# Turning both quantised activations by DMA in a fused attention and FP4 feed-forward kernel

## What is computed

```python
def fp4_quant_dequant(x):
    xb = x.reshape(shape[:-1] + (shape[-1] // BLOCK, BLOCK))
    scale = jnp.maximum(jnp.max(jnp.abs(xb), axis=-1, keepdims=True) / 6.0, 1e-12)
    idx = jnp.searchsorted(_MID, jnp.abs(xb / scale))
    return (_GRID[idx] * jnp.sign(xb / scale) * scale).reshape(shape)
...
# attention: a decaying linear attention, chunked in the reference
v = out32 @ W_write.T
intra = einsum(S * M, v)        # S[i, j] = x[i] . x[j-1], M = decay and causal mask
x = _layernorm(x + out + alpha * (reads @ W_read.T))
# feed-forward, each matmul on quantised operands; H = 256, I = 704
gate, y = fp4_linear(x, w_gate), fp4_linear(x, w_up)
h = jax.nn.silu(gate) * y
x = _layernorm(x + fp4_linear(h, w_down))
```

## Time and profile before

| | |
|---|---|
| median of 3 runs | 324.36 us (324.16 to 324.38) |
| span of the profiled execution | 322.5 us |
| PE, PEld busy | 314.5 us (97%), 285.2 us (88%) |
| DVE busy | 293.0 us (91%) |
| POOL busy | 238.2 us (74%) |
| ACT busy | 213.2 us (66%) |
| DMA | 15.7 MB, 14% of the 16 engines' time |
| granted TensorE clock | full in all 40 slices |

### The profile page before, as it was taken

One profiled execution on the slowest core, in us unless ns is written; L12 is line 12 of the kernel. 1 busy time (PEld: TensorE's weight loads), 2 busy tenths in 40 slices (PEclk: granted clock), 3 DMA queues, 4 the chain that ended last, 5 costly groups with the idle time before them and its releaser, 6 DMA issues.

```text
span 322.5 us, 6519 instructions
## 1 busy us (share of the span) xinstructions
PE 314.5 (97%) x2067; PEld 285.2 (88%) x2067; DVE 293.0 (91%) x746; ACT 213.2 (66%) x521; POOL 238.2 (74%) x258
## 2 busy tenths in 40 slices
PE   7999999999999999999999999999999999999994
PEld 3999988989998998999989998898989889998983
DVE  4799789989899999899998999889999999999973
ACT  7769994767775647844784556766675555665664
POOL 1999898668696868676886768777779588368872
PEclk9999999999999999999999999999999999999999
DMA  6830301010010200320020200021000000001002
GB/s 227 302 125 9 132 0 67 1 66 2 1 67 16 84 16 0 100 82 3 16 83 17 83 17 3 33 65 35 1 18 17 16 18 17 19 16 35 17 33 84
DMA packets 8242, 15.69 MB, mean 49 GB/s; under 512 B 1040, under 2 KB 5136, under 8 KB 8208
## 3 DMA queue, kind: packets, MB, share of 16 engines
q1 hardware_dynamic: 7920, 15.01, 14.0%
q10 hardware_dynamic: 288, 0.26, 0.3%
HBM read 11.08 MB, written 4.19 MB: 47 GB/s over the span
## 4 chain that ended last, share of the span: by engine, by line
PE 69%; DVE 17%; issue 5%; ACT 4%; POOL 3%; ACTq 0%; DVEq 0%; POOLq 0%
PE gu L1712 11%; PE gu L1716 11%; PE gu L1713 11%; PE bank L1817 5%; PE bank L1712 4%; PE bank L1716 4%; PE bank L1713 4%; PE bank L1722 3%; DVE h_y L1094 3%; PE bank L1725 3%; PE bank L1726 3%; DVE w_raw L1209 2%; DVE hqT_lo L1236 2%; DVE h_am L1215 2%; PE bank L1783 2%
## 5 line engine op out<-in xcount | busy, mean ns | idle before, releaser
L413 POOL TENSOR_TENSOR h_q<-h_g,h_ns 128x704 f32<-128x704 f32 x32 | 51.2, 1604 | 47.7 <-DVE h_g L1099 47.6
L1712 PE MATMUL gu<-guT_hi,xqT_hi 128*128 128x512 f32 (+1 forms) x192 | 74.0, 386 | 0.7 <-DVE w_raw L1209 0.6
L1713 PE MATMUL gu<-guT_lo,xqT_hi 128*128 128x512 f32 (+1 forms) x192 | 72.2, 376 | 0.0
L1716 PE MATMUL gu<-guT_hi,xqT_lo 128*128 128x512 f32 (+1 forms) x192 | 56.6, 376 | 0.0
L699 ACT ACTIVATE w_raw<-gu 128x512 f32<-128x512 f32 x64 | 29.3, 462 | 32.7 <-PE gu L1716 32.4
L406 POOL TENSOR_TENSOR h_n<-w_raw,h_rs 128x704 f32<-128x704 f32 x32 | 47.0, 1472 | 3.4 <-DVE h_rs L1089 3.2
L719 ACT CAST hqT_hi<-bank 128x512 fp32r<-128x512 f32 x64 | 30.4, 478 | 17.7 <-PE bank L1817 17.2
L1712 PEld LDWEIGHTS gu<-guT_hi,xqT_hi 128*128 128x128 f32 x192 | 36.1, 188 | 6.0 <-ACT xqT_hi L688 0.9
L1716 PEld LDWEIGHTS gu<-guT_hi,xqT_lo 128*128 128x128 f32 x192 | 35.5, 188 | 6.0 <-ACT xqT_lo L693 0.2
L1713 PEld LDWEIGHTS gu<-guT_lo,xqT_hi 128*128 128x128 f32 x192 | 36.1, 188 | 4.8
L1094 DVE SCALAR_TENSOR_TENSOR h_y<-h_sq,h_n 128x704 f32<-128x704 bf16 x34 | 36.9, 1090 | 0.0
(11 more groups left out here) (159 smaller groups left out, 936.7 us busy)
## 6 DMA issues: line engine op xcount, KB each, us to landing
xs<-in_x_rows_dram SPq DMA_DIRECT2D x8, 512.0 KB, 3.4
out_dram<-wq_gu SPq DMA_DIRECT2D x32, 128.0 KB, 1.7
x_full<-in_xt_rows_dram SPq DMA_DIRECT2D x7, 512.0 KB, 3.2
w_raw<-in_w_ffn_dram SPq DMA_DIRECT2D x6, 352.0 KB, 6.0
w_pair<-in_w_attn_dram SPq DMA_DIRECT2D x1, 512.0 KB, 5.2
x_full<-in_xt_rows_dram SPq DMA_DIRECT2D x1, 256.0 KB, 2.6
x_full<-in_xt_rows_dram ACTq DMA_DIRECT2D x1, 256.0 KB, 3.4
scal<-in_scalars_dram ACTq DMA_DIRECT2D x1, 1.0 KB, 1.7
```

The lines of the kernel that those rows point to most:

```text
L413: nc.gpsimd.tensor_tensor(blocks(h_q[:, p, 0:I]), blocks(h_g[:, p, :]), per_block(h_ns[:, p, :], HB), ALU.mult).then_inc(h_quant, 1)
L1712: nc.tensor.matmul(dst, lh, rh, start=(first and i == 0), stop=False)
L1713: nc.tensor.matmul(dst, lh, rl, start=False, stop=False)
L1716: last = nc.tensor.matmul(dst, ll, rh, start=False, stop=(end and i == len(terms) - 1))
```

## The change

1. **Grids turned by DMA.** The grid values that `x_to_grid` and `h_to_grid` make are now bfloat16 (`x_g`, `h_g`). For all x and for h of tiles 0 to 29, SP issues a transposing DMA from `x_g` or `h_g` to `x_gT` or `h_gT`. The block scales (`x_ns`, `h_ns`) go their own way: PE transposes them in one instruction (`x_scale_rows`, `h_scale_rows`: 40 or 56 rows), ACT copies them from PSUM (`copy_x_scales`, `copy_h_scales`), SP writes them to DRAM and reads them back with each row repeated over 16 partitions (`x_sT`, `h_sT`). POOL multiplies grid by scales already in the turned layout (`x_spread`, `h_spread`), and ACT and DVE round and subtract from SBUF, over 768 columns at once for h (`h_round_all`, `h_rest_all`). Tiles 30 and 31 still go through `h_dequant` and `h_transpose`.
2. **Squares in PSUM.** `x_squares`, `h_squares` and `w_squares` write float32 to PSUM banks; the two DVE helpers read them there.
3. **Scale rows of odd length**, padded to 5 and 7 groups (`XC`, `SC`), and `x_moments` works on one column at a time (four instructions in place of two). `out_moments` leaves `o_nm` out; POOL folds it into `o_shift`.
4. **The last scores block of a batch** (j = 3, 128 columns) is two plain float32 matmuls on `x_full` in place of six fp32r ones; the next load of `x_full` waits for it.
5. **v and x rests** of the first batches are always made by DVE; `v_subtract`, `xq_subtract` and the ACT copies behind them are gone.
6. **Everything is reordered**: PSUM banks by tables indexed by batch or tile, no loop body, a new list on every engine. `gate_up` waits for `silu_ready` first and for `h_ready` before its second bank.

```diff
-            def v_subtract(n, u):
-            def xq_transpose(n, u, free):
-            def xq_subtract(n, u):
+        s_at = ((6, 3, 5, 4),
...
+            def write_h_scales(k, p, turn):
+                sp.wait_ge(hs_copied, k + 1)
+                sp.dma_start(h_scales_dram[k], h_s[:, p, :]).then_inc(hs_written[p], 16)
+            def spread_h_scales(k, p, turn):
+                sp.wait_ge(hs_written[p], 16 * turn)
+                if turn > 1:
+                    sp.wait_ge(h_quant, k - 1)
+                sp.dma_start(h_sT[:, p, :], over_rows(h_scales_dram[k], SC, HC)).then_inc(hs_landed[p], 16)
+            def turn_h_grid(k, p, turn):
+                sp.wait_ge(hg_repeated, k + 1)
+                if turn > 1:
+                    sp.wait_ge(h_quant, k - 1)
+                sp.dma_start_transpose(h_gT[:, p, :, :], h_g[:, p, :]).then_inc(hg_turned[p], 16)
...
             def load_x_transposed(n):
                 sp.wait_ge(xT_lo_ready, 2 * n)
+                sp.wait_ge(s_filled, 4 * n)
...
+            def h_spread(k, p, turn):
+                pool.wait_ge(hs_landed[p], 16 * turn)
+                pool.wait_ge(hg_turned[p], 16 * turn)
...
+                nc.gpsimd.tensor_tensor(h_q[:, p, :], h_gT[:, p, :, :].rearrange("p c t -> p (c t)"), h_sT[:, p, :],
+                                        ALU.mult).then_inc(h_quant, 1)
...
-                nc.scalar.activation(h_sq[:, p, :], h_n[:, p, :], ACT.Square, scale=ROOT_K).then_inc(h_square, 1)
+                nc.scalar.activation(two_banks(h_sq_at[k]), halves(h_n[:, p, :]), ACT.Square,
+                                     scale=ROOT_K).then_inc(h_square, 1)
...
-                nc.vector.tensor_scalar(z_nm[:, c], z_sum[:, c], -1.0 / D, None, ALU.mult)
...
+                for i in (2 * u, 2 * u + 1):
+                    nc.vector.tensor_scalar(z_nm[:, i:i + 1], z_sum[:, i:i + 1], -1.0 / D, None, ALU.mult)
...
+            def h_rest_all(k, p):
+                dve.wait_ge(hT_hi_ready, 2 * k + 2)
+                nc.vector.tensor_tensor(hqT_lo[:, p, :], h_q[:, p, :], hqT_hi[:, p, :].bitcast(F32),
+                                        ALU.subtract).then_inc(hT_lo_ready, 2)
...
+                if j == TILES - 1:
+                    prev, cur = slice(j * P - 1, (j + 1) * P - 1), slice(j * P, T)
+                    for dk in range(DK):
+                        last = nc.tensor.matmul(ps[:, s_at[n][j], 0:P], x_full[:, dk, prev], x_full[:, dk, cur],
+                                                start=(dk == 0), stop=(dk == DK - 1))
...
+            def h_scale_rows(k, p, free):
+                pe.wait_ge(hs_repeated, k + 1)
+                wait_all(free)
+                nc.tensor.transpose(ps[0:SROWS, hs_at[k], 0:P], h_ns[:, p, :], ident[:]).then_inc(hs_filled, 1)
```

More of the change, by code:

```diff
@@ new lines, in _ @@
+            decay_scores(3, 2)
+            h_magic_add(4, 0)
+            h_reciprocals(6, 0)
+            h_rest_all(0, 0)
+            h_magic_add(5, 1)
+            h_rest_all(1, 1)
+            hidden(7, 1, 0)
+            hidden(7, 1, 1)
+            v_rest(3, 1)
+            h_maxima(7, 1)
+            h_to_grid(4, 0)
+            h_to_grid(5, 1)
+            h_divisors(7, 1)
+            h_reciprocals(7, 1)
+            x_residual(3, 0)
+            hidden(8, 0, 0)
+            hidden(8, 0, 1)
@@ new lines, in _ @@
+            h_to_grid(8, 0)
+            v_rest(4, 0)
+            h_magic_add(9, 1)
+            h_to_grid(9, 1)
+            x_maxima(3, 1)
+            x_residual(4, 0)
+            x_divisors(3, 1)
+            hidden(11, 1, 0)
+            x_reciprocals(3, 1)
+            xq_rest(3, 0)
+            x_moments(4, 0)
+            hidden(11, 1, 1)
+            out_residual(2, 2)
+            h_maxima(11, 1)
+            x_magic_add(3, 1)
+            out_moments(2, 0)
+            h_rest_all(4, 0)
@@ new lines, in _ @@
+            x_moments(4, 1)
+            out_residual(4, 0)
+            xq_rest(3, 1)
+            hidden(12, 0, 0)
+            hidden(12, 0, 1)
+            h_magic_add(10, 0)
+            h_maxima(12, 0)
+            h_to_grid(10, 0)
+            out_moments(4, 0)
+            h_divisors(12, 0)
+            h_reciprocals(12, 0)
+            hidden(13, 1, 0)
+            decay_scores(5, 0)
+            h_magic_add(11, 1)
+            x_maxima(4, 1)
+            hidden(13, 1, 1)
+            x_divisors(4, 1)
@@ new lines, in _ @@
+            out_residual(6, 2)
+            h_reciprocals(14, 0)
+            h_rest_all(8, 0)
+            xq_rest(4, 0)
+            h_to_grid(12, 0)
+            v_rest(5, 0)
+            out_moments(6, 0)
+            hidden(15, 1, 0)
+            v_rest(5, 1)
+            hidden(15, 1, 1)
+            x_residual(5, 0)
+            h_maxima(15, 1)
+            decay_scores(5, 2)
+            h_magic_add(13, 1)
+            x_moments(5, 0)
+            h_to_grid(13, 1)
+            hidden(16, 0, 0)
```

2523 lines of the change are left out of this document (1502 added, 1021 removed).

## The result

The changed kernel takes 354.19 us (351.41 to 354.80) where the kernel before, on the same chip, takes 324.37: a ratio of 1.090, 95% interval 1.086 to 1.094. It is 29.8 us slower, where 302 was predicted. The profiled execution has a span of 352.8 us. All times are medians of a kernel's executions, and where one execution was over 1.5% slower than the kernel's fastest, the median without it is 0.2 to 1.5 us lower (loads first 349.5, split scores block 350.0, no turns 326.3, no round trip 318.8, writes by ACT 350.0).

What follows compares the result with a forecast made beforehand. PE was taken to bound the kernel, with DVE leading after the change: DVE busy 286.3, with idle start and end 299.4, plus 1 between, plus 1.9 to the runs' median, gave 302 us; range 295 to 316.

Steps and rivals of the forecast that it cites:

- PE's work: On PE, removed and added transposes, scores block and subtractions sum to -25.0 us, up to -28 with small ones.
- the bound's 0.1 us for a change of kind: On PE, 46 scale transposes might each also pay about 0.1 us between other matmuls: +10 instead of +5.1.
- The new contacts: On DVE, 46 subtractions now reading two SBUF operands wait on POOL, 0.27 us each: +12.4 us.
- The squares' term: On DVE, squares in PSUM take away the waits on POOL in the passes for h and x: -14.7 us.
- DVE leads: The forecast case: DVE's busy time plus its idle time sets the span, giving 302 us; chance 0.48.
- slack towards PE: DVE's 16.4 us of idle time between start and end, expected to shrink to 0.5 to 2 us.
- PE leads: Rival: DVE's contacts stay near 4 us and PE sets a span of 295 to 297.5, time 298; chance 0.17.
- SP and DMA: Turns land in 3 us, scales' write and read take 1.7 + 2.6; no cost while DVE's distance covers them.
- The load of `x_full` ... covered by the batch's `gate_up`s: On SP, this load now waits for the fourth scores block; its 3 us were to be hidden behind gate_up work.
- The turns are late: Rival: at 5 us a half of x comes 2 us late, some six of 16 halves, 12 us: 314; chance 0.15.
- The rival of serial turns: Transposing DMAs run one after another, each as slow as the slowest load: 331 us; chance 0.10.
- the three signs named: Signs against the forecast: DVE's or POOL's largest wait for a DMA, PE gaps over 10 us, first gate_up later.

Runs made afterwards that it cites:

- loads first: Changed kernel with the second batch's load of x_full put behind four weight loads and the load of xs in SP's list: 350.16 us.
- split scores block: Changed kernel with each batch's last scores block as split terms again, so no load of x_full waits for the fourth block: 350.21 us.
- no turns: Changed kernel with x_full's second load behind the other loads and all 46 transposing DMAs left out: 326.79 us.
- no round trip: Changed kernel with x_full's second load behind the other loads and the scales' 46 DRAM writes and 46 reads left out: 320.32 us.
- writes by ACT: Changed kernel with x_full's second load behind the other loads and the 46 scale-row writes issued by ACT, not SP: 351.23 us.
- the kernel that comes nearest (316.55): Changed kernel with x_full's second load moved back, an eighth of the scale reads' bytes, and the old last scores block without its wait: 316.55 us.

## Why the prediction was wrong

**PE's work: right but for 7 us.** The sum said -25. With the turns and the round trip left out PE is busy for 296.6 us, 17.9 less than before. With each matmul counted from its start to the start of the next (or to its end, where PE then stands idle), the terms compare like this (us):

| term | predicted | measured |
|---|---|---|
| transposes of h gone | -19.8 | -16.0 |
| transposes of x gone | -7.0 | -6.4 |
| transposes of scales added | +5.1 | +3.3 |
| last scores block | -1.6 | -1.1 |
| subtractions for v and x gone | -1.7 (x not counted) | -2.1 |
| all other matmuls | 0 | +4.4 |

The transposes of h were priced too high: the 0.66 us of six run to the end of the last one, but the next matmul starts 0.03 us after the last one has started. One that stands alone between two other matmuls adds 0.03 us in the median, for h and x alike, so no run shows the bound's 0.1 us for a change of kind either. Of the last row some 3 us are clock: PE ran 6.5 us of its busy time at the lower level of 1.2 GHz (0.91 granted in each of the first two stretches of 20 us, where it was 1.00 before). The plain scores block was priced well: 0.60 us to its end, but 0.36 to 0.40 until the next matmul starts in six of the eight batches, where the split one took 0.62; in the first two batches PE stands idle behind it.

**DVE and POOL: right in busy time.** 286.3 was forecast, 281.6 measured and 279 to 285 in the experiments that keep the squares in PSUM; POOL 241.9 for 238 to 248. The passes are at 880 and 876 ns without long ones. The new contacts cost less than the 12.4:

```profile
L1681 DVE TENSOR_TENSOR hqT_lo<-h_q,hqT_hi 128x768 fp32r<-128x768 f32 x30 | 32.2, 1078 | 5.8 <-ACT hqT_hi L1001 5.8
```

The median of that group is 950 ns, so 30 x 0.128 = 3.8 us, and with 3.6 for x (908 in the mean, 684 the median, 16 of them) 7.4 together. The squares' term, -14.7, was right in kind; undoing it adds 33 us to DVE's busy time and 42 to the kernel's.

**The step "DVE leads": wrong by 15 us, even without any DMA trouble.** The prediction took DVE's 286.3, added its idle time at the start and the end and left "0.5 to 2" for all between. In the kernel that comes nearest (316.55) DVE is idle for 18.4 us between 40 and 280, where PE has only 3.6 us of gaps: PE leads. The idle time that the prediction called slack towards PE, 16.4 us before, did not shrink. PE's own idle time is 17.6 us, 7.0 of it in the first 40 us and over 7 behind 280, against 8.0 in all before. The rival "PE leads" had the right engine and 298. Its span of 297.5 falls short of the profiled 316.4 by 9.3 us of PE's work (298.8 busy, not 289.5) and 9.6 of idle time, which it took from the kernel before; the profiled execution is the slowest of this kernel, 1.6 us above its median.

**The step "SP and DMA": the one that turned a gain into a loss, 30 us** (350.16 with the full reads, 320.26 with an eighth)**.** "I take 3 us" for a turn was right for a turn alone: 2.8 for h, 2.3 for x. "The scales' write and read back, 1.7 + 2.6" and "Cost: nothing while DVE's distance covers it" priced each transfer from rows of a kernel whose DMA engines were 14% busy. No term was made for what 384 KB read beside each turn would do: the added bytes could have been counted, 30 x 384 + 16 x 256 KB = 16.0 MB, as much again as the whole kernel moved. The trace before also held a warning that the prediction read the other way ("plain ones issued close together land together"): the six loads that SP issues from 6.66 us on, 0.37 to 0.49 us apart, land at 9.9, 11.1, 13.4, 14.3, 15.2 and 16.1 us. The first takes 3.2 us from issue to landing, the last 7.1. The list, which the prediction did price, costs nothing.

**The step "The load of `x_full` ... covered by the batch's `gate_up`s": wrong, 4 us here and 6.8 alone.** The first batch has no `gate_up` in front of it, and the loads behind it in SP's list were not looked at. The prediction asked what stands behind a wait in SP's list for the scale reads ("with turns and stores queued behind it"), and not for this one.

Together these account for the 52.2 us between 302 and 354.19: 14.6 for the engines' own pace (316.55), 3.7 for the wait of `x_full` once the reads are small (320.26), 29.9 for the reads beside the turns (350.16) and 4.0 for the loads behind that wait at the start.

**The rivals.** "The turns are late" named the mechanism and sized it from the turns alone, 12 us and not 30. The rival of serial turns, "Slower than before", had the direction and not the cause. Of the three signs named, two held: the first `gate_up` starts at 46.3 us, not 40.5, and PE's gaps between 20 and 280 us add up to 27.6. The sign on DMA waits would have misled: summed up, POOL's largest wait is for DVE and DVE's for ACT, and the DMA waits come after them (though DVE's longest single one, 7.71 us, is for the load of `xs`), since in a ring of waits the engine named need not be the one to blame. Of what the forecast itself asked to see, PE was busy for 306.4 us and not near 288, DVE for 80% of the span and not 95%, and the turned grids of h landed in 4.4 us and not within 3.

In a sentence of its own: the 1309 ns for a 128x128 DMA transpose (Trainium skill, VectorE: DVE Perf Modes, section "The three transpose paths") don't add up block by block, since six blocks land in 2.7 us at the least and 4.4 in the median; that the rival made of 7.9 us, 363, is the number nearest to 354 is luck, for the turns are not what takes the time.

## What to carry to other kernels

Price a transfer that is added beside others by what it brings to the DMA engines, bytes and the number of rows that it walks, and not by the landing time of a like one in a quiet trace; a broadcast read counts with the bytes that it writes (16 MB more moved here, for scale rows of 1.2 MB). When one wait is added to an in-order list, read on down the list for what now stands behind it, above all in the start, where all loads are. And when leaving out either of two things gives the same gain as leaving out both, look for what they do to each other.

## What was not expected of the hardware

- DMA transposes and large broadcast reads slow each other: occupied time of an engine 45 us for the turns, 57 for the scales, 135 for both, by the differences to the kernel with neither.
- The same 384 KB, read as 16 rows to 8 partitions each and not as 8 rows to 16, made the kernel 15.8 us faster.
- Half of the bytes, read from 4 rows, left three quarters of the loss of the whole, read from 8 (343.4, 350.2 and, with an eighth, 320.3 us).
- A DMA transpose holds SP's queue for 1.2 us, where the plain DMAs of the changed kernel hold it for 0.3 to 0.6 in the median of their kind, and with short reads this cost nothing.
- Six plain loads issued 0.37 to 0.49 us apart landed 0.8 to 2.4 us apart, the last 7.1 us after its issue.
- PE's granted clock fell to 0.74 in the mean over a stretch of 20 us in which PE stood idle for 7.58 us in one piece.
